# Eleven late node tiles behind the edge pairs of layer 2, expert weights split in place, a new buffer map

## The chip, the cores and the metric

One core of one Trainium2 chip. The metric is the device time of one execution in microseconds (us). Its engines are TensorE (PE, matrix products), VectorE (DVE), ScalarE (ACT), GpSimd (POOL) and SyncE (SP, which only issues transfers here); 16 DMA engines move data between DRAM and SBUF.

## The reference

Two layers of a gated relational graph network over 10000 nodes of 512 features and 5000 edges, then a mixture of experts over the nodes:

```python
for r in range(2):                                  # two relations, w[r] = sum_b att[r, b] * basis[b]
    gate = sigmoid(x_j @ gate_w[r])                 # x_j = x[dst], one row per edge
    msgs.append(gate[:, None] * x_j @ w[r])
msg = where(edge_type == 0, msgs[0], msgs[1])
layer(x) = segment_sum(msg, src) + x @ root + bias
y = relu(layer1(layernorm(x)));  z = layer2(y);  x = x + z
out = x + shared_experts(layernorm(x)) + sum over top 2 of 8 routed experts(layernorm(x))
```

All products are made in about full float32 precision from high and low halves: hi x hi, lo x hi and hi x lo, three matrix instructions per block of 128 of the inner size.

## The kernel before

The nodes are 79 tiles of 128 rows (`NT`; the last is the tail of the 10000 rows and overlaps the one before it). The edges, sorted by relation, are 42 tiles in 21 pairs (`NPAIR`). The five engine programs are written out in order and meet in semaphores. The stages are:

- A: node tiles 0 to 73 of layer 1. Each is normalised, transposed by PE, split (`hi` on ACT, `lo` on DVE), multiplied by the root weights, and `y_out` (DVE) adds the bias into `yout`, which SP stores to the table y1 in DRAM, two tiles in a transfer.
- B: the 21 edge pairs of layer 1. POOL gathers 256 rows (`gather`, L766), ACT and DVE make the gate and the gated halves, PE turns them with a matrix that sums the rows of equal source in the pair (L1119), multiplies by the relation's weights, ACT writes `message`, and POOL scatters it onto y1 with an accumulating indirect transfer (`scatter`, L781). A pair's scatters wait until the pair before it has landed, and a message waits for the scatter two pairs back.
- late A: node tiles 74 to 78 of layer 1 behind the pairs. Their rows of y1 are set to zero at the start; POOL adds the tiles to them with accumulating transfers (L819, L822) once all scatters have landed.
- C: all 79 node tiles of layer 2 (input y1, output stored to the table z), and D: the 21 edge pairs of layer 2, scattered onto z.
- the groups: 20 groups of 512 nodes (the last has 384). SP loads z and x, POOL (`add_x`; for group 0 DVE) adds them, DVE and POOL make the moments, ACT normalises (`q_norm`), PE transposes, ACT and DVE split (`q_hi`, `q_lo`), PE makes router logits, hidden layer and output.

In A and C, one relation weight chunk out of 32 is formed on every second tile from a basis load of 960 KB (`load_basis`, `w_rows`, `w_evac`), goes to DRAM (`store_w`), comes back in two loads into `wrl` and is split at tiles 68 to 71 (`W_SPLIT_AT`, `w_hi`, `w_lo`). In the last steps of A and C (`LEADS`) the first pairs of the next stage are prepared.

Behind D, the kernel loads the two expert weights (1280 KB each) into a staging buffer that takes the place of `xin` and `yout`, ACT and DVE split them in the last five pairs of D and behind it, DVE makes the bias rows (L1541 to L1545) and the router's tables (L1549 to L1558), and every engine waits for all scatters of D (`scattered`). SP issues the loads of x groups 0 and 1 (1024 KB each) right behind the expert weights, at the start of D, and those of z behind the scatters.

Chunks are counted from 0 to 63 over both layers; chunk 34 is the third of layer 2.

Of the kernel before, what the change touches and what calls it, by code (L numbers as in the profile page):

```python
# [20 lines left out]
F32 = mybir.dt.float32  # L21
# [7 lines left out]
P = 128  # L29
# [32 lines left out]
def gnn_moe_kernel(nc, x, src, dst, etype, basis, att, gate_w, root, bias,  # L62
# [3 lines left out]
    KC = H // P  # L66
    NB = basis[0].shape[0]
# [18 lines left out]
    TURN_AT, REPEATS_AT, W_SPLIT_AT = 34, 42, 68  # L86
# [3 lines left out]
    QT = 4  # L90
    QLAST = 3
    LATE = 5
    NA = NT - LATE
    assert NA % 2 == 0 and LATE < 8
    A0, B0, L0, C0, D0 = 0, NA, NA + ET, NT + ET, 2 * NT + ET
    SA, SB, SL, SC, SD = "A", "B", "late A", "C", "D"
    NSTORE = [16 * ((NA // 2 + 1) // 2), 16 * (NA // 4)]

# [8 lines left out]
    with ctx:  # L107
# [75 lines left out]
        w2h, e3 = place("w2h", [P, FC, H], F32R, at=e2)  # L183
        w2l, e4 = place("w2l", [P, FC, H], F32R, at=e3)
# [15 lines left out]
        assert s1 <= top[0]  # L200
        xy_at = top[0]
        xin = sb("xin", [P, 4, 2, H])
        yout = sb("yout", [P, 2, 2, H])
        stage_w1, s3 = place("stage_w1", [P, KC, FH], at=xy_at)
        stage_w2, s4 = place("stage_w2", [P, FC, H], at=s3)
        assert s4 <= top[0]
# [4 lines left out]
        xn_e = sb("xn_e", [P, 4, H])  # L211
        eh, el = sb("eh", [P, 2, H], F32R), sb("el", [P, 2, H], F32R)
        same = sb("same", [P, 2, 2, PW], F32R)
        msg = sb("msg", [P, 4, H])
        stage1, s2 = place("stage1", [P, KC, H], at=xe_at)
        assert s2 <= top[0]
        scratch = sb("scratch", [P, H])
# [3 lines left out]
        top[0] = late  # L221
        xr = sb("xr", [P, 2, QT, H])
        assert top[0] <= root2_end
        zr = sb("zr", [P, 4, QT, H])
        tn = sb("tn", [P, QT, H])
        tth, ttl = sb("tth", [P, 2, KC, QT * P], F32R), sb("ttl", [P, 2, KC, QT * P], F32R)
        gel = sb("gel", [P, 2, QT * P])
        gsc = sb("gsc", [P, 2, QT * P])
        gth, gtl = sb("gth", [P, FC, QT * P], F32R), sb("gtl", [P, FC, QT * P], F32R)
        cwt = sb("cwt", [P, 2, QT * P], F32R)  # L230
        gwp = sb("gwp", [P, KC, P], F32R)
        lgs = sb("lgs", [P, QT, NE])
        lgt = sb("lgt", [P, QT * P])
# [17 lines left out]
        assert top[0] <= nc.sbuf_usable_end, (top[0], nc.sbuf_usable_end)  # L251
# [42 lines left out]
        s_late = sem("late_rows_added")  # L294
# [68 lines left out]
        def phase_of(S):  # L363
            for name, t0, t1 in ((SA, 0, NA), (SL, NA, NT), (SC, 0, NT)):
                if START[name] + t0 <= S < START[name] + t1:
                    return name, S - START[name]
# [1347 lines left out]
```

## Time and profile before

| what | value |
| --- | --- |
| median of 3 runs | 1699.88 us (1698.68 to 1703.02) |
| profiled execution, its time | 1702.22 us |
| profiled execution, its span | 1700.5 us |
| PE busy | 1586.2 us, 93% of the span |
| DVE, ACT, POOL busy | 911.4, 725.0, 510.6 us |
| moved by DMA | 271.47 MB, mean 160 GB/s |

The span is the time between the first and the last instruction of the profile. Busy times of different engines overlap; only what lies on the chain that ends last makes the time. Matrix instructions overlap as well: one of 512 columns is busy for 0.39 us, but one starts every 0.23 us.

### The profile page before, as it was taken

The page shows a single profiled execution, that of the slowest core. Times are in us where ns is not written, and L with a number is a line of the kernel's source. Part 1 is how long each engine was busy: PE and PEld are TensorE (multiplying, and loading weights), DVE is VectorE, ACT ScalarE, POOL GpSimd, SP SyncE. Part 2 cuts the span into 40 slices and gives each one's busy share as a digit, 9 for nine tenths or more (in the row PEclk, how much of TensorE's full clock was granted, in tenths as well). Part 3 has the DMA queues.
Part 4 walks back from the last instruction along what each step waited for, and adds up shares of the span by engine and source line. Part 5 has one row for each costly group of instructions (what it writes and reads, how often), then busy time and mean ns, then how long its engine had stood idle before and what let it go on. Part 6 is the DMA issues. An engine that isn't in the chain of part 4 may idle for free. (4 is left out here: it accounts for less than half of the span.)

```text
span 1700.5 us, 23999 instructions
## 1 busy us (share of the span) xinstructions
PE 1586.2 (93%) x7903; PEld 1253.3 (74%) x7903; DVE 911.4 (54%) x2179; ACT 725.0 (43%) x1168; POOL 510.6 (30%) x562
## 2 busy tenths in 40 slices
PE   3998999998998999999999818999999999999998
PEld 2676766787786777778888616888888888888887
DVE  3554686877732333335665436555556555655543
ACT  2343444666631222223665514444444444443542
POOL 3682232477732000000467433122112211221100
PEclk9999999999999999999999959999999999999999
DMA  8997999576759999994777650231122112211201
GB/s 243 281 284 227 304 299 284 157 134 123 130 68 276 284 280 280 276 283 162 214 128 131 92 173 0 102 121 75 75 105 119 74 74 109 114 74 74 87 26 44
DMA packets 72773, 271.47 MB, mean 160 GB/s; under 512 B 12550, under 2 KB 12564, under 8 KB 57570
## 3 DMA queue, kind: packets, MB, share of 16 engines
q1 hardware_dynamic: 51922, 223.59, 41.6%
q0 software_dynamic: 20752, 46.65, 15.0%
q8 instruction: 50, 0.82, 0.2%
q14 instruction: 49, 0.40, 0.1%
HBM read 179.82 MB, written 90.34 MB: 159 GB/s over the span
## 5 line engine op out<-in xcount | busy, mean ns | idle before, releaser
L848 POOL TENSOR_TENSOR zr<-zr,xr 128x2048 f32<-128x2048 f32 (+1 forms) x19 | 89.2, 4699 | 395.6 <-DMA xr<-in_x 395.1
L879 ACT ACTIVATE th<-bank 128x512 fp32r<-128x512 f32 x158 | 94.4, 597 | 185.8 <-PE bank L1106 185.5
L1086 PE MATMUL bank<-tth,w1h 128*128 128x512 f32 (+1 forms) x400 | 164.0, 410 | 0.1
L1086 PE MATMUL bank<-ttl,w1h 128*128 128x512 f32 (+1 forms) x400 | 156.5, 391 | 0.0
L1086 PE MATMUL bank<-tth,w1l 128*128 128x512 f32 (+1 forms) x400 | 155.4, 388 | 0.0
L1086 PE MATMUL bank<-w2h,gth 128*128 128x512 f32 x395 | 155.2, 393 | 0.0
L1086 PE MATMUL bank<-w2h,gtl 128*128 128x512 f32 x395 | 154.7, 392 | 0.0
L1086 PE MATMUL bank<-w2l,gth 128*128 128x512 f32 x395 | 154.3, 391 | 0.0
L1362 DVE SCALAR_TENSOR_TENSOR tl<-bank,th 128x512 fp32r<-128x512 f32 x79 | 54.7, 692 | 179.2 <-ACT th L879 179.1
L1086 PE MATMUL bank<-root1h,th 128*128 128x512 f32 x316 | 133.4, 422 | 5.9 <-DVE yout L1384 4.2
L766 POOL DMA_INDIRECT gx<-y,dst_slot x42 | 45.5, 1084 | 297.0 <-ACT xn_e L899 274.4
L1086 PE MATMUL bank<-root2h,th 128*128 128x512 f32 x316 | 131.9, 417 | 1.8 <-DVE yout L1384 1.2
L1086 PE MATMUL bank<-root1l,th 128*128 128x512 f32 x316 | 126.4, 400 | 0.0
L1086 PE MATMUL bank<-root1h,tl 128*128 128x512 f32 x316 | 125.4, 397 | 0.0
L1086 PE MATMUL bank<-root2l,th 128*128 128x512 f32 x316 | 125.0, 396 | 0.0
L1086 PE MATMUL bank<-root2h,tl 128*128 128x512 f32 x316 | 123.9, 392 | 0.0
L922 ACT ACTIVATE wevac<-bank 128x512 f32<-128x512 f32 x64 | 38.2, 597 | 183.2 <-PE bank L1157 183.2
L1384 DVE TENSOR_TENSOR yout<-bank,bias_b 128x512 f32<-128x512 f32 x157 | 107.1, 682 | 14.1 <-PE bank L1086 5.8
L1020 ACT ACTIVATE gel<-bank,b 128x512 f32<-128x512 f32 (+1 forms) x100 | 68.3, 683 | 108.3 <-PE bank L1086 108.2
L1365 DVE TENSOR_TENSOR tl<-bank,th 128x512 fp32r<-128x512 f32 x79 | 54.5, 690 | 111.3 <-ACT th L879 110.6
L1119 PE MATMUL bank<-same,eh 128*128 128x256 f32 x336 | 83.6, 287 | 12.3 <-issue 8.5
L1590 DVE TENSOR_TENSOR gtl<-gsc,gth 128x512 fp32r<-128x512 f32 (+1 forms) x80 | 79.3, 992 | 21.7 <-ACT gth L1032 16.3
(204 smaller groups left out, 3790.0 us busy)
## 6 DMA issues: line engine op xcount, KB each, us to landing
basis_t<-in_gnn_basis SPq DMA_DIRECT2D x64, 896.0 KB
xin<-in_x SPq DMA_DIRECT2D x39, 512.0 KB, 8.7
xin<-y SPq DMA_DIRECT2D x39, 512.0 KB, 6.5
z<-yout SPq DMA_DIRECT2D x39, 512.0 KB, 6.9
xr<-in_x SPq DMA_DIRECT2D x19, 1024.0 KB, 6.8
zr<-z SPq DMA_DIRECT2D x19, 1024.0 KB, 4.8
out<-zr SPq DMA_DIRECT2D x19, 1024.0 KB, 3.9
y<-yout SPq DMA_DIRECT2D x37, 512.0 KB, 9.2
```

Of the source, the lines that this page charges most:

```text
L766: pool.indirect_dma_start(out=gx[:, e % 6, :], out_offset=None, in_=x if pr.phase == SB else y1, in_offset=bass.IndirectOffsetOnAxis(ap=ds ...
L848: pool.tensor_tensor(zq, zq, xr[:, q.mod(2), 0:n, :], ALU.add).then_inc(s_zx, 1)
L879: act.activation(th_a[:, s, :], tpb[s][:], f).then_inc(s_hi, 1)
L922: act.activation(wevac[:, u.mod(2), c.mod(2), :], wb[c.mod(2)][:], ACT.Copy).then_inc(s_wv, 1)
L1020: act.activation(gel[:, u % 2, 0:n], outb[u % 2][:, 0:n], ACT.Gelu, bias=b1[:, c:c + 1]).then_inc(s_ge, 1)
L1086: ins = pe.matmul(out_ap, a(k), b(k), start=first, stop=last)
L1119: pe.matmul(o, eh[:, j, k * P:(k + 1) * P], m, start=j == 0, stop=False)
L1362: ins = dve.scalar_tensor_tensor(out=tl_a[:, s, :], in0=tpb[s][:], scalar=0.0, in1=th_a[:, s, :].bitcast(F32), op0=ALU.max, op1=ALU.subtract)
L1365: ins = dve.tensor_tensor(tl_a[:, s, :], tpb[s][:], th_a[:, s, :].bitcast(F32), ALU.subtract)
L1384: dve.tensor_tensor(target, outb[st.T.mod(2)][:], bias_b[st.layer][:], ALU.add).then_inc(s_y, 1)
L1590: dve.tensor_tensor(gtl[:, c, 0:n], source, gth[:, c, 0:n].bitcast(F32), ALU.subtract).then_inc(s_gl, 1)
```

## The change

Layer 2 now treats its last tiles as layer 1 does, but eleven of them (tiles 68 to 78, stage E, `late2_steps`). Stage C ends with tile 67. E's tiles are transposed and multiplied behind the pairs of D, and their results are written to four pair buffers (two of `yout`, `xn_a`, a new `late_out`; the fifth pair takes the first again once its transfer has landed; the tail goes to `scratch`). POOL adds them to z with five accumulating transfers of 512 KB and one of 32 KB. The rows of z from 8704 on, which get only such additions, are zeroed by 13 transfers issued by SP behind stage A and the first basis loads of layer 2. Two of layer 2's weight chunks are formed before C (`FORMED`), the other 30 on its first 60 tiles, and the split moves to tiles 64 to 67. The expert weights are loaded into the places of `w1l` and `w2h` and split there, w1 in D's last five pairs and w2 in E's first five tiles; bias rows, router tables, the addition of x to z for group 0 and its moments stand in DVE's program behind tiles 5, 6, 7 and 8 of E (counted from 0). SP issues x loads 0 and 1 once the last edge rows of D are gated. The group buffers get new places, so that they don't overlap what E still uses.

```diff
-    LATE = 5
-    NA = NT - LATE
+    LATE, LATE2 = 5, 11
+    NA, NC = NT - LATE, NT - LATE2
+    FORMED = [0, 2]
-    TURN_AT, REPEATS_AT, W_SPLIT_AT = 34, 42, 68
+    TURN_AT, REPEATS_AT, W_SPLIT_AT = 34, 42, [68, 64]
-        w2h, e3 = place("w2h", [P, FC, H], F32R, at=e2)
-        w2l, e4 = place("w2l", [P, FC, H], F32R, at=e3)
+        w2l, e3 = place("w2l", [P, FC, H], F32R, at=e2)
+        w2h, e4 = place("w2h", [P, FC, H], F32R, at=e3)
+        stage_w1, _ = place("stage_w1", [P, KC, FH], at=e1)
+        stage_w2, _ = place("stage_w2", [P, FC, H], at=e2)
-        zero_rows = [(y1, r) for r in range(NA * P, N + PW, P)] + [(z, r) for r in range(N, N + PW, P)]
+        zero_rows = [[(y1, r) for r in range(NA * P, N + PW, P)], [(z, r) for r in range(NC * P, N + PW, P)]]
+        late2_steps = [Step(SE, Pos(t)) for t in range(NC, NT)]
+        LATE2_PAIRS = range(NC // 2, NG)
+        def late2_buffer(g):
+            k = (g - NC // 2) % 4
+            return (yout[:, k % 2, :, :], k) if k < 2 else ((xn_a, late_out)[k - 2][:, :, :], k)
+        def late2_added(eng):
+            for k in range(5):
+                eng.wait_ge(s_late2[k], 16 * (len(LATE2_PAIRS[k::4]) if k < 4 else 1))
 # SP
+                    for c in range(FORMED[1]):
+                        sp.wait_ge(s_w, CS + c + 1)
+                        load_basis(1, Pos(c + 2))
+                    store_w(1, Pos(0))
             for c in range(2):
                 load_basis(1, Pos(c))
+            zero_late_rows(1)
             walk(sp, SC, step)
 ...
                 sp.wait_ge(s_mm, D0)
-                for i in range(2):
-                    sp.wait_ge(s_ystore[i], stored(i, 1))
 ...
+            sp.wait_ge(s_xn, 2 * ET)
+            sp.wait_ge(s_el, 2 * ET)
             for q in range(2):
                 load_x(Pos(q))
+            for g in range(NG - 1, NG + 1):
+                sp.wait_ge(s_tp, Step(SE, Pos(2 * (g - 4) + 1)).T.k + 1)
+                load_pair(SE, Pos(g))
             scattered(sp, 1)
             for q in range(2):
                 load_z(Pos(q))
             load_group(Pos(2))
+            late2_added(sp)
 # POOL, behind edges(SD) and scattered(pool, 1)
+            def add_late2(g):
+                rows, k = late2_buffer(g)
+                pool.wait_ge(s_y, NT + 2 * g + 2)
+                pool.dma_start(pair_rows(z, Pos(g), 2), rows, accum_op=ALU.add).then_inc(s_late2[k], 16)
+            for g in LATE2_PAIRS[:4]:
+                add_late2(g)
             group_rstd(Pos(0))
             add_x(Pos(1))
+            for g in LATE2_PAIRS[4:]:
+                add_late2(g)
+            pool.wait_ge(s_y, 2 * NT)
+            pool.dma_start(z[TAIL + again:N, :], scratch[again:P, :], accum_op=ALU.add).then_inc(s_late2[4], 16)
             group_rstd(Pos(1))
 # ACT
+            for c in range(FORMED[1]):
+                w_evac(Pos(CS + c))
             hi(Step(SC, Pos(0)))
 ...
+            hi(late2_steps[0])
             message(Pair(SD, NPAIR - 1), 1)
-            scattered(act, 1)
+            for i in range(LATE2):
+                if i + 1 < LATE2:
+                    hi(late2_steps[i + 1])
+                if i < FC:
+                    expert_hi(FC + i)
             q_norm(Pos(0))
+            late2_added(act)
             for k in range(KC):
                 q_hi(Pos(0), k)
 # PE
+            for c in range(FORMED[1]):
+                w_rows(Pos(CS + c), 1)
             transpose(Step(SC, Pos(0)))
 ...
+            transpose(late2_steps[0])
+            for st in late2_steps:
+                if not is_tail(st):
+                    transpose(Step(SE, st.t + 1))
+                multiply(st)
             scattered(pe, 1)
+            pe.wait_ge(s_y, 2 * NT)
             pe.wait_ge(s_ewl, 2 * FC)
             pe.wait_ge(s_qs, 1)
 # DVE
+                if st.phase == SE and st.g.k - 4 in LATE2_PAIRS and not apart:
+                    dve.wait_ge(s_late2[0], 16)
 ...
-            dve.wait_ge(s_mm, D0 + ET)
-            for n in range(FC, 2 * FC):
-                expert_lo(n)
 ...
+            lo(late2_steps[0])
+            for i, st in enumerate(late2_steps):
+                if not is_tail(st):
+                    lo(Step(SE, st.t + 1))
+                y_out(st)
+                if i < FC:
+                    expert_lo(FC + i)
+                elif i == FC:
+                    bias_rows()
+                elif i == FC + 1:
+                    router_tiles()
+                elif i == FC + 2:
+                    add_first()
+                elif i == FC + 3:
+                    q_stats(Pos(0), range(QT), True)
+            late2_added(dve)
             for k in range(KC):
                 q_lo(Pos(0), k)
```

## Rows read from the trace of the kernel before

**Rows 1.** The page's head: span and instructions.
```profile
span 1700.5 us, 23999 instructions
```

**Rows 2.** Chain that ended last, 930 to 1060 us: start, us, what.
```profile
989.15 5.16 DMA z<-msg,scat_slot
...
994.37 5.67 DMA zr<-z
...
1012.54 0.61 ACT tth L1013
```

**Rows 3.** Waits of PE, 800 to 1060 us: in total, times, longest.
```profile
PE bank L1213 <- ACT tn L1004: 38.4, 2, 36.9
```

**Rows 4.** Windows: length, busy PE, PEld, DVE, ACT, POOL; clock; DMA share; GB/s.
```profile
980.00:990.00 10.00, 0.00 (x0) 0.00 (x0) 1.01 (x2) 0.00 (x0) 4.93 (x4) 0.50 0.52 58
```

**Rows 5.** Timeline of DVE, stage C: start, us, line, operation, [idle before].
```profile
740.36 0.68 DVE L1384 TENSOR_TENSOR yout<-bank,bias_b 128x512 f32<-128x512 f32 x1
...
747.92 0.68 DVE L1384 TENSOR_TENSOR yout<-bank,bias_b 128x512 f32<-128x512 f32 x1
...
783.29 0.68 DVE L1384 TENSOR_TENSOR yout<-bank,bias_b 128x512 f32<-128x512 f32 x1
...
802.51 0.68 DVE L1384 TENSOR_TENSOR yout<-bank,bias_b 128x512 f32<-128x512 f32 x1
```

**Rows 6.** Timeline of POOL: a pair's first scatter, stages B and D.
```profile
335.93 1.68 POOL L781 DMA_INDIRECT y<-msg,scat_slot  x1 [0.31 <-issue]
...
354.35 1.64 POOL L781 DMA_INDIRECT y<-msg,scat_slot  x1 [1.13 <-issue]
...
504.26 1.55 POOL L781 DMA_INDIRECT y<-msg,scat_slot  x1 [4.54 <-issue]
...
819.13 1.64 POOL L781 DMA_INDIRECT z<-msg,scat_slot  x1 [4.73 <-DMA z<-yout]
...
841.83 1.63 POOL L781 DMA_INDIRECT z<-msg,scat_slot  x1 [4.25 <-issue]
...
987.28 1.56 POOL L781 DMA_INDIRECT z<-msg,scat_slot  x1 [4.46 <-issue]
```

**Rows 7.** C's start: a window as in rows 4, and the DMA list's tail add.
```profile
520.00:523.00 3.00, 3.00 (x15) 2.42 (x15) 0.18 (x1) 0.60 (x1) 0.00 (x0) 0.88 1.07 277
...
y<-xn_e POOLq DMA_DIRECT2D x1, 32.0 KB, 13.5
```

**Rows 8.** Timeline of SP's queue, start of D.
```profile
818.40 0.40 SPq L567 DMA_DIRECT2D stage_w<-in_w1T  x1
...
819.40 1.07 SPq L633 DMA_DIRECT2D xr<-in_x  x2
```

**Rows 9.** Timeline of ACT, end of D: the last pair's first message.
```profile
976.03 0.60 ACT L915 ACTIVATE msg<-bank 128x512 f32<-128x512 f32 x1 [4.89 <-DMA z<-msg,scat_slot]
```

**Rows 10.** Timeline of DVE behind D.
```profile
978.39 0.42 DVE L1541 CAST b2r<-b 128x512 fp32r<-128x512 f32 x1
...
980.30 0.75 DVE L1544 SCALAR_TENSOR_TENSOR b2r<-b2lo,lo_row,b2r 128x512 fp32r<-128x512 f32 x1
...
994.47 0.09 DVE L1549 MEMSET topv<- 128x32 f32 x1 [13.42 <-DMA z<-msg,scat_slot]
...
996.26 0.09 DVE L1558 MEMSET cw<- 128x40 f32 x1
...
1000.17 2.50 DVE L1671 TENSOR_TENSOR zr<-zr,xr 128x512 f32<-128x512 f32 x4 [3.82 <-DMA zr<-z]
...
1005.21 0.38 DVE L1571 BATCH_NORM_AGGREGATE qmv<-qbn 128x2 f32<-128x6 f32 x4
```

**Rows 11.** Timeline of POOL: z plus x of group 1.
```profile
1008.19 4.51 POOL L848 TENSOR_TENSOR zr<-zr,xr 128x2048 f32<-128x2048 f32 x1
```

**Rows 12.** Chain that ended last: the same piece of two groups in a row.
```profile
1054.26 3.45 PE bank L1086 x15
...
1088.12 3.45 PE bank L1086 x15
```

More of the change, by code:

```diff
@@ L66, in gnn_moe_kernel @@
     KC = H // P
+    QT = 4
     NB = basis[0].shape[0]
@@ L294, in gnn_moe_kernel @@
         s_late = sem("late_rows_added")
+        s_late2 = [sem(f"late_rows_added{i}") for i in range(5)]
         s_gx = [sem(f"gathered{i}") for i in range(6)]
@@ L367, in phase_of @@
             return None, 0
[L369 to L370 removed]
+        START = {SA: A0, SB: B0, SL: L0 - NA, SC: C0, SD: D0, SE: E0 - NC}
+        NODES_BEFORE = {SA: 0, SL: 0, SC: NT, SE: NT}
         PAIRS_BEFORE = {SB: 0, SD: NPAIR}
[L372 to L373 removed]
+        LAYER = {SA: 0, SB: 0, SL: 0, SC: 1, SD: 1, SE: 1}
+        LAST = {SA: NA - 1, SC: NC - 1}
+        STORES = [[(n // 2 + 1 - i) // 2 for i in range(2)] for n in (NA, NC)]
         def stored(i, layer):
[L377 removed]
+            return 16 * sum(STORES[l][i] for l in range(layer + 1))
         def buffer_free(i, gg):
[L381 removed]
+            return gg.div(2).times(16, 16 * (STORES[0][i] - (NG + 1) // 2) if gg.k > NG else 0)
         class Step:
@@ L551, in store_pair, with zero_late_rows @@
                 wait(sp, s_y, n)
-                if tiles == 1:
-                    before_gg = gg + (-1)
-                    sp.wait_ge(s_ystore[before_gg.mod(2)], buffer_free(before_gg.mod(2), before_gg) + 16)
                 table = y1 if phase == SA else z
+                assert tiles == 2
                 sp.dma_start(pair_rows(table, g, tiles), yout[:, gg.mod(2), 0:tiles, :]).then_inc(s_ystore[gg.mod(2)], 16)
+            def zero_late_rows(layer):
+                for table, r in zero_rows[layer]:
+                    n = min(P, N + PW - r)
+                    sp.dma_start(table[r:r + n, :], zeros[0:n, :]).then_inc(s_zero_rows, 16)
             def flush_stores(phase):
@@ L773, in scatter @@
                         pool.wait_ge(s_sidx, 1)
-                        pool.wait_ge(s_zero_rows, 16 * zero_stores)
+                    pool.wait_ge(s_zero_rows, 16 * sum(len(zero_rows[l]) for l in range(pr.layer + 1)))
                     for i in range(2):
@@ new lines, in router_tiles @@
+            def router_tiles():
+                scattered(dve, 1)
+                dve.memset(topv[:], -1.0)
+                for k in range(KC):
+                    dve.tensor_copy(gwp[:, k, :], zeros[:, 0:P])
+                for i in range(2):
+                    ins = dve.tensor_copy(cwt[:, i, :], zeros[:])
+                link(ins)
+                link(dve.tensor_copy(gwp[:, :, 0:NE], gw[:]))
+                dve.tensor_tensor(gwp[:, :, NE:2 * NE], gw[:], gwp[:, :, 0:NE].bitcast(F32), ALU.subtract)
+                dve.memset(cw3[:, :, 0:2, :], 1.0)
+                dve.memset(cw3[:, :, 2, :], 0.0).then_inc(s_qs, 1)
+                dve.wait_ge(s_qs, 1)
```

159 lines of the change are left out of this document (72 added, 87 removed).

## The prediction, made before the result was known

> **What bounds the kernel now.** I began with the page's span and engine totals [rows 1] and then followed the chain that ended last from its end. The chain is TensorE (PE) work back to 1012.54 us, and before that a row of scatters into z, ending with the one issued at 989.15 that takes 5.16 us; then the first z load, 5.67 us [rows 2]. The waits say what PE did meanwhile: one wait of 36.9 us ahead of the first router transposes [rows 3], and the window inside it shows no PE work and the clock at 0.50, the lower of its two levels [rows 4]. So there are two kinds of stretch. Node tiles (stage C) and expert groups are bound by PE: two C tiles with a weight chunk take 747.92 - 740.36 = 7.56 us, six without one 802.51 - 783.29 = 19.22, or 3.20 each [rows 5]. Edge pairs (stages B, D) are bound by the scatter queue: 18 periods from 354.35 to 504.26 are 8.33 us each, 18 from 841.83 to 987.28 are 8.08 [rows 6], each the landing of the last scatter plus the issue of the next. What PE has to do in the shadow of that queue is free; what disturbs the queue's transfers is paid in full.
>
> All times below are in the profiled execution: span 1700.5, its own time 1702.22, so 1.7 lies around the span. The median of the runs is 1699.88, 2.3 under the profiled time; I carry the difference over.
>
> **Stage C loses eleven tiles.** 11 x 3.20 = 35.2 us come off PE before stage D [rows 5]; everything from D to its last scatter moves forward by that. The places of the lead steps and of the weight split hang on the end of C and move with it; load and split of the last weight rows keep their three tiles of distance. The split now ends on C's last tile, before the first pair, where seven tiles lay between. DVE's two subtractions there come ahead of its work for pair 0, but that waits for PE's turns anyway: nothing, at worst 1.3 us.
>
> **Two chunks formed before C.** Each costs PE 7.56 - 6.40 = 1.16, and they land where PE waits at the layer change, so up to -2.3. But SP also issues their successors' loads (960 KB each, 2.0 MB together) some 12 us earlier, into the stretch in which the y loads and the three accumulating transfers already fill the engines (share 1.07 and 277 GB/s) and in which the last of those adds takes 13.5 us to land [rows 7]. 2.0 MB at 277 GB/s is 7.1 us of queue. Chunk 34's load must be there one tile after C starts, and bias additions of C wait for the adds. Bounds of the stall: 0 (it fits in the time PE spends on tiles 0 and 1) and 7.1; I take 3.0, since only part of the queue stands ahead of what is waited for.
>
> **Thirteen zero stores.** z from row 8704 on is zeroed: 3.2 MB behind stage B's first pairs (before, two transfers of z were zeroed at the kernel's start, where they cost nothing visible). How much bulk traffic slows the scatter queue has two rows. In B, 2.0 MB of basis loads run beside the first two periods, which take 354.35 - 335.93 = 18.4, 1.8 over two normal ones. In D, the expert weights and x groups 0 and 1 (4.7 MB) are issued at 818.4 to 820.5 [rows 8], and the first two periods take 841.83 - 819.13 = 22.7, 6.5 over [rows 6]. That is 0.9 to 1.4 us per MB; 3.2 MB give 2.9 to 4.5. I take +4.2; the bounds are 0 and 11.5 (queue stopped for 3.2 MB at 277 GB/s). No slack gives it back: the next periods are latency.
>
> **x loads moved to the end of D.** SP no longer issues them at the start of D: 2.1 MB x 1.4 = -3.0. It issues them when the last edge rows are gated, about 958.5 in old time, with five scatters to go: +3.0. Net 0, bounds -3 and +3. Dropping SP's wait for the last store ahead of the expert loads moves them by under 2 us. Expert splitting in place halves ScalarE's and VectorE's work per pair in D, which is hidden there.
>
> **Eleven late tiles.** In old time, D's last but one message is at 976.03 [rows 9]; with one expert split, hi and lo behind it PE starts the first late product at 978.5 and ends tile i at 981.4 + 3.2 i. VectorE (DVE) has 1.4 us of its own per tile, plus 0.7 of expert split up to tile 4, bias rows behind tile 5 (978.39 to 981.05: 2.7), router tables behind tile 6 (1.9), z plus x behind tile 7 (2.5) and the moments of group 0 behind tile 8 (2.9) [rows 10]. Played through in order, DVE falls behind PE from tile 7 on: y of tile 8 is written at 1009.5, the moments stand at Q = 1012.4 instead of 1005.6, tile 10's product ends at 1015.9 instead of 1013.4. The waits put in between should be met: the scatters end at 994.3, z's first load lands 5.7 (rows 2) to 13.5 later, 1008.0 at worst against 1005.7 when it is read; the first add, whose buffer tile 8 takes, lands by 1008 if it takes as long as in layer 1.
>
> **What ScalarE and DVE wait for now.** GpSimd (POOL) runs: adds 0 to 3, rstd of group 0, z plus x of group 1, add 4, tail add. rstd ends 2.65 after Q (1005.60 to about 1008.2), at 1015.0; the addition takes 4.5 [rows 11] to 1019.6; two issues bring the last to 1020.9. The first turned group may be written to SBUF only when all adds have landed. PE can do just two transposed banks before. Landing, bounds: 4.8 (a scatter with nothing beside it; 5.16 in rows 2) and 13.5 (layer 1 with its bulk loads, rows 7). Here SP has nothing queued but z and x of group 2, issued 12 us earlier, so I take 5.6: 1026.5. Against 1012.54 [rows 2] that is +14.0, with ends of +13.2 and +21.9.
>
> The Trainium skill ("DMA: Bandwidth & Descriptors", section "Anatomy of one DMA — SWDGE (gpsimd) path") puts a GpSimd transfer at about 2.0 us plus bytes at 436 GB/s, 3.2 us for 512 KB. By that page the wait would end near 1024 and the sum would be some 2.5 us lower. Rows 7's 13.5 us for 32 KB shows it is no bound beside other traffic.
>
> Behind that, router start-up and groups are the same instructions; the clock was low there before and is again after the short gap.
>
> **Sum.** -35.2 (tiles) - 2.3 (chunks) + 3.0 (crowding at C's start) + 4.2 (zeros) - 3.0 + 3.0 (x loads) + 14.0 (start of the router) = -16.3. Profiled time 1702.2 - 16.3 = 1685.9; median 1699.9 - 16.3 = 1683.6, say 1684.
>
> **Rivals.**
> A. The transfers are hidden: zeros and crowding cost 0, x loads gain 3 at D's start and cost nothing at its end: -35.2 - 2.3 - 3.0 + 13.2 = -27.3, median 1673. For it: the C stage has PE busy throughout although DMA is near full. Against: both first-period rows of the scatter queue.
> B. The transfers cost what the crowded rows say: crowding 7.1, last adds 13.5: -35.2 - 2.3 + 7.1 + 4.2 + 21.9 = -4.3, median 1696. For it: rows 7. Against: nothing bulky is queued beside the last adds.
> C. Slower than before: the new buffer map makes the steady expert groups slower, for example through operands of PE, DVE and POOL that now lie elsewhere. A group takes 1088.12 - 1054.26 = 33.86 with PE never idle [rows 12], and there are 20. With -16.3 elsewhere it decides from 0.82 us per group on; at 1.0 it gives +20 - 16.3, median 1704. Against it: PE, the bound, has only its instruction stream to spend there, and that is unchanged.
> D. The change doesn't do what it says: late tiles don't run beside the scatters because a product waits (for y of tile 8 and its buffer, or for the scatter wait in DVE's tables). If the four tiles from tile 7 on waited till behind the adds, 4 x 3.2 = 12.8 would come back: -3.5, median 1696. DVE's order makes a part of this likely (2.5 us is in the sum), not all.
>
> **How the numbers follow.** Forecast 0.58 (its own range 1678 to 1691); A 0.20; B 0.09; D 0.07; C 0.06. A measurement of this kernel tells about 0.3% (5 us) from no change. Slower: C, 0.06. Within 0.3% (over 1694.8): B and D reach their price only when several bounds meet, so half of each, 0.08. Faster 0.86. The range 1670 to 1696 takes in A and B at their own values and leaves out C, the far side of B and D and what lies below A, together under 0.2.
>
> **What would show it.** PE's long wait ahead of the router transposes falls from 36.9 to a few us, followed by a new one of 6 to 9 us before the transposed group's first split, released by the adds. B's first three scatter periods grow by about 4 us in sum; D's first two shrink by 3. C starts with a PE wait for a basis chunk or for y, 3 us. Late tiles run 3.2 us apart up to tile 6. The forecast fails if scatter periods in B stay long after the zeros, if C shows waits for basis throughout, if the last adds take 13 us, or if the group period isn't 33.86.

## The result, and the profile after

| what | before | after |
| --- | --- | --- |
| median of 17 runs each, us | 1701.43 (1695.84 to 1706.84) | 1695.01 (1682.36 to 1701.80) |
| ratio of the times | | 0.9954 (0.9941 to 0.9967) |
| profiled execution: its time, its span | 1702.22, 1700.5 | 1694.41, 1692.7 |

The change is faster, by 0.46% or 7.8 us; 16.3 us had been forecast. The sign was right, the size twice too large. The same kernel against the same kernel before in a second session gave 0.9941 (0.992 to 0.9962), 10.0 us.

The head of the page after, then POOL's timeline with the scatters that answer to [rows 6]: first scatter of the first, third and last pair of B, and the same of D.

```profile
span 1692.7 us, 24017 instructions
```
```profile
335.11 1.68 POOL L814 DMA_INDIRECT y<-msg,scat_slot  x1 [0.20 <-issue]
...
356.88 1.64 POOL L814 DMA_INDIRECT y<-msg,scat_slot  x1 [3.36 <-issue]
...
503.05 1.55 POOL L814 DMA_INDIRECT y<-msg,scat_slot  x1 [4.25 <-issue]
...
791.02 1.63 POOL L814 DMA_INDIRECT z<-msg,scat_slot  x1 [5.50 <-issue]
...
810.03 1.62 POOL L814 DMA_INDIRECT z<-msg,scat_slot  x1 [1.75 <-issue]
...
958.35 1.55 POOL L814 DMA_INDIRECT z<-msg,scat_slot  x1 [4.32 <-issue]
```

These six starts, ACT's first split of the transposed group 0 (the tth of [rows 2]), DVE's subtraction `gtl` that opens the second group, and the span cut every kernel of this study into the same stretches. D0 is the first pair of stage D, "last" the last pair:

| kernel | span | B: first to third | B: third to last | B last to D0 | D0 to D last | D last to split | split to group | groups |
| --- | --- | --- | --- | --- | --- | --- | --- | --- |
| before | 1700.5 | 18.4 | 149.9 | 314.9 | 168.2 | 25.3 | 57.1 | 630.8 |
| before, once more | 1700.0 | 19.4 | 147.8 | 317.0 | 165.2 | 25.1 | 58.6 | 632.0 |
| gate_before | 1698.2 | 18.8 | 149.6 | 315.8 | 166.4 | 25.2 | 57.5 | 630.8 |
| after | 1692.7 | 21.8 | 146.2 | 288.0 | 167.3 | 40.4 | 59.0 | 634.9 |
| after, once more | 1686.2 | 22.3 | 147.2 | 286.0 | 165.7 | 39.1 | 59.0 | 631.9 |
| gate_after | 1690.4 | 22.5 | 148.7 | 285.5 | 166.5 | 39.1 | 57.5 | 630.8 |
| zeros_early | 1697.8 | 18.7 | 150.8 | 287.9 | 166.6 | 37.6 | 61.7 | 632.8 |
| early_chunks | 1691.0 | 23.4 | 155.0 | 280.8 | 166.5 | 38.8 | 58.9 | 632.3 |
| adds_first | 1685.2 | 22.6 | 144.3 | 285.6 | 167.2 | 35.9 | 59.5 | 632.5 |
| seven_tiles | 1688.3 | 19.6 | 146.5 | 295.5 | 169.3 | 29.8 | 59.1 | 631.9 |
| seven_with_chunks | 1689.6 | 19.7 | 147.9 | 298.4 | 167.6 | 27.8 | 59.2 | 631.3 |
| x_behind | 1689.5 | 22.1 | 147.4 | 286.1 | 165.2 | 38.5 | 59.1 | 634.1 |
| adds_first_gate | 1693.6 | 22.9 | 151.0 | 289.7 | 168.3 | 33.7 | 57.3 | 630.8 |
| all_three | 1687.5 | 23.2 | 148.0 | 288.0 | 165.4 | 38.6 | 56.3 | 630.8 |
| wait_back | 1695.3 | 22.7 | 146.5 | 288.6 | 170.5 | 37.0 | 61.7 | 632.9 |
| adds_first_gate_wait | 1686.9 | 23.0 | 149.7 | 287.8 | 168.3 | 34.6 | 56.7 | 630.7 |

What lies ahead of B is not in the table. It was 334.1 to 335.9 us in the three profiles of the program before, 335.0 to 339.9 in twelve of changed programs and 341.7 in zeros_early, the only one that adds transfers there. So a single span says little and the stretches say more; whether the changed programs really lose a little ahead of B, and to what, stays open. In the first pair of profiles: up to B's last pair -1.2, B to D0 -26.9, D -0.8, the tail +15.1, the first group +1.9, the others +4.1; the sum is the 7.8 us.

**The tail.** The chain that ended last, in the stretch of [rows 2]; then PE's waits, 760 to 1060 us, where [rows 3] had 36.9 in one (columns: total, times, longest).

```profile
988.66 4.49 POOL zr L886
993.15 0.60 POOL z L867
993.75 4.82 DMA z<-scratch
...
998.75 0.61 ACT tth L1053
...
1003.61 3.78 PE bank L1296 x8
```
```profile
PE bank L1268 <- DVE ttl L1632: 7.4, 1, 7.4
```

The long wait is gone, and the one forecast in its place stands there: POOL's addition of z and x, the last two adds behind it, and 4.82 us until the last has landed. From D's last pair to the split it is 40.4, 39.1 and 39.1 us in after, again_after and gate_after; before 25.3, 25.1 and 25.2. That is +14.4, forecast +14.0. Three more programs keep this order of adds and x loads: zeros_early has 37.6, early_chunks 38.8, wait_back 37.0, so +12 to +15 is as much as can be said.

**The start of C.** PE's waits from 505 to 560 us, after:

```profile
PE bank L1205 <- DMA basis_t<-in_gnn_basis: 5.3, 1, 5.3
PE bank L1152 <- DMA xin<-y: 2.3, 1, 2.3
```

before, the same stretch:

```profile
PE bank L1106 <- DMA xin<-y: 4.0, 1, 4.0
```

and a window (columns as in [rows 4]), after, then before:

```profile
526.00:532.00 6.00, 3.10 (x13) 1.44 (x14) 0.69 (x1) 0.68 (x2) 4.56 (x5) 0.50 0.96 202
```
```profile
526.00:532.00 6.00, 5.32 (x27) 4.28 (x27) 2.70 (x5) 1.72 (x3) 4.30 (x5) 1.00 0.87 202
```

PE waits for a basis chunk, for which it did not wait before, and in the pause the granted clock falls to 0.50, the lower level (1.2 GHz), where before it was at 1.00. It is a second fall rather than a new kind of one: at 514 to 520 us the clock was 0.50 before and 0.72 after. Behind the pause the chunk's eight matrix instructions take 1.93 us, before 1.07. DVE's timeline has the cost in one number. The eighth tile of C is written at 551.44 before and 556.37 after:

```profile
551.44 0.68 DVE L1384 TENSOR_TENSOR yout<-bank,bias_b 128x512 f32<-128x512 f32 x1
...
815.57 0.68 DVE L1384 TENSOR_TENSOR yout<-bank,bias_b 128x512 f32<-128x512 f32 x1
```
```profile
556.37 0.68 DVE L1446 TENSOR_TENSOR yout<-bank,bias_b 128x512 f32<-128x512 f32 x1
...
786.27 0.68 DVE L1446 TENSOR_TENSOR yout<-bank,bias_b 128x512 f32<-128x512 f32 x1
```

Counted from B's last pair that is 47.2 and 53.3 us. The three profiles of the program before average 48.2 (47.2 to 49.3), the seven with eleven tiles, zeros and chunks as in the change 53.3 (52.8 to 53.8; after, once more, gate_after, adds_first, x_behind, adds_first_gate, all_three). The two programs with the wait put back, the same up to there, have 54.0 and 52.6. The second row of each is C's last tile: the first scatter of D comes 3.56 us after it before (819.13 - 815.57, and 3.56 in all three profiles), 4.75 after.

### The profile page after: what moved, and what is told of

Its sections match the earlier page's. It is cut to its first block and busy times, and to the rows that moved or that the text cites. A ratio compares the mean times of both kernels' runs of the same rounds, so it can differ in the third digit from the quotient of the medians.

```text
span 1692.7 us, 24017 instructions
## 1 busy us (share of the span) xinstructions
PE 1595.1 (94%) x7903; PEld 1258.1 (74%) x7903; DVE 919.8 (54%) x2179; ACT 723.9 (43%) x1168; POOL 513.5 (30%) x568
## 5 line engine op out<-in xcount | busy, mean ns | idle before, releaser
L1446 DVE TENSOR_TENSOR yout<-bank,bias_b 128x512 f32<-128x512 f32 x152 | 103.7, 682 | 31.5 <-PE bank L1132 14.4
L1646 DVE TENSOR_TENSOR gtl<-gsc,gth 128x512 fp32r<-128x512 f32 (+1 forms) x80 | 87.0, 1087 | 21.7 <-ACT gth L1072 16.3
```

Of the source, the lines that this page charges most:

```text
L1446: dve.tensor_tensor(target, outb[st.T.mod(2)][:], bias_b[st.layer][:], ALU.add).then_inc(s_y, 1)
L1646: dve.tensor_tensor(gtl[:, c, 0:n], source, gth[:, c, 0:n].bitcast(F32), ALU.subtract).then_inc(s_gl, 1)
```

## The experiments

There were fourteen more runs. The two called again are the two programs unchanged, measured a second time. Every row of the table is one execution: that of adds_first_gate took 1695.37 us, the longest of its five, 10 us over their median.

**again_after, again_before**: no edit.

> The changed kernel itself, a second time, to see which of the losses in its first profile come back. Theory 1 (port race): the groups lose time where GpSimd's addition of z and x starts just ahead of VectorE's subtraction gtl<-gsc,gth; which of the two comes first changes from run to run, so the number of groups longer than 33.86 us is another one here (0 to 6) and the stage from the first split tth to the end differs from the first profile's 693.95 us by 1 to 5 us. Theory 2 (buffer map): the new places make groups longer; then the same groups are long by the same amounts. For the start of stage C, both expect PE's wait for a basis chunk again, 4 to 6 us. Ratio 0.994 to 0.997.

> The kernel before a second time, for its profile. Theory 1: one or more groups longer than 33.86 us are possible here too, since only the landing of an x load decides. Theory 2: all groups 33.86 us again. Stage C's start without a wait for a basis chunk, the scatter queue of stage B from its first to its last start 170 us within 2.

Measured: 1691.42 us, ratio 0.9941 (0.992 to 0.9962); the program before 1701.78 in its one execution, beside a median of 1701.47 of its runs in that session. The stretches that come again are the stretch to D0 and the tail. The group stretch was 634.9 and is 631.9: a part of the first profile's loss there comes and goes. B of the program before, first to last pair, took 167.2 us, a little less than the 168 to 172 expected.

**gate_after, gate_before**: POOL adds x to the group three ahead only once the router weights of the next group are known, in either program.

```diff
-                if not missing(q + 3):
-                    add_x(q + 3)
                 if not missing(q + 2):
                     group_rstd(q + 2)
+                if not missing(q + 3):
+                    wait(pool, s_cw3, q.times(1, 2))
+                    add_x(q + 3)
```

> Changed kernel, but GpSimd adds x to z of group q+3 only once the router weights of group q+1 are known, where VectorE has no operation with two SBUF inputs of 512 columns. Theory 1 (port race): no group is longer than 33.86 us, gtl takes 0.69 us everywhere in the loop, the time falls 3 to 5 us against the changed kernel in the same job. Theory 2 (buffer map): the groups stay as long as they were, same time. Rival 3: the later addition makes moments or loads late and costs 1 us or more in every group, slower by 20.

> The kernel before with the same gate on GpSimd's addition. Theory 1: gain of 0 to 3 us, since in its profile no group lost more than 0.1 us but other executions may lose some; its spread over rounds shrinks. Theory 2: no change. Rival 3: slower by 20.

Why this place: in the first profile after, two subtractions of DVE that mostly take 0.69 us took 4.17 and 5.15. DVE's timeline:

```profile
1068.55 4.17 DVE L1646 TENSOR_TENSOR gtl<-gsc,gth 128x512 fp32r<-128x512 f32 x1
...
1100.10 5.15 DVE L1646 TENSOR_TENSOR gtl<-gsc,gth 128x512 fp32r<-128x512 f32 x1
...
1107.14 0.69 DVE L1646 TENSOR_TENSOR gtl<-gsc,gth 128x512 fp32r<-128x512 f32 x1
```

and POOL's, the same stretch:

```profile
1067.56 4.62 POOL L886 TENSOR_TENSOR zr<-zr,xr 128x2048 f32<-128x2048 f32 x1 [28.15 <-DMA xr<-in_x]
...
1100.09 4.61 POOL L886 TENSOR_TENSOR zr<-zr,xr 128x2048 f32<-128x2048 f32 x1 [23.56 <-DMA xr<-in_x]
```

Both times POOL's addition had begun just before, 0.99 and 0.01 us, and DVE's subtraction ended when POOL's was over (1067.56 + 4.62 = 1072.18 against 1068.55 + 4.17 = 1072.72; 1104.70 against 1105.25). The Trainium skill says so ("SBUF — State Buffer", section "SBUF: two separate sides"): a DVE operation with two inputs in SBUF and a GpSimd operation that reads SBUF exclude each other for a whole instruction; the rows agree. Gated, POOL's timeline in gate_after is

```profile
1082.78 4.61 POOL L887 TENSOR_TENSOR zr<-zr,xr 128x2048 f32<-128x2048 f32 x1 [7.70 <-DVEq L1696]
...
1116.64 4.62 POOL L887 TENSOR_TENSOR zr<-zr,xr 128x2048 f32<-128x2048 f32 x1 [7.70 <-DVEq L1696]
```

one group apart (33.86, as in [rows 12]), and the groups take 630.8 us in each gated profile, one of before and four of changed programs (630.7 to 630.8), against 630.8 and 632.0 ungated before and 631.3 to 634.9 in nine ungated profiles of changed programs. So the buffer map costs the groups nothing: what is left is where POOL's addition happens to fall, which hangs on when x lands (its releaser in the row). Ratios: gate_after 0.993 (0.9904 to 0.9955), gate_before 0.9985 (0.9968 to 1.0002). In its session gate_after has 1689.36 us and the changed program 1691.42; 3 to 5 us had been expected, and the two intervals overlap. So the gate's effect is shown in the group stretch, not in the time.

**zeros_early**: the thirteen zero stores are issued at the kernel's start with the others.

```diff
             zero_late_rows(0)
+            zero_late_rows(1)
 ...
-            zero_late_rows(1)
```

> Changed kernel, with the 13 zero transfers to z issued at the kernel's start. Theory 1 (they disturb B's first scatters, but B catches up later): the first two periods of B's scatter queue fall from 22 to 19 us, the following 18 grow from 147 to 149, and B's end moves by 1.5 us or less. Rival (my prediction): B gets 3 to 4 us shorter.

POOL's timeline, first pair, third and last of B:

```profile
341.67 1.67 POOL L814 DMA_INDIRECT y<-msg,scat_slot  x1 [0.20 <-issue]
...
360.37 1.64 POOL L814 DMA_INDIRECT y<-msg,scat_slot  x1 [1.29 <-issue]
...
511.14 1.55 POOL L814 DMA_INDIRECT y<-msg,scat_slot  x1 [4.49 <-issue]
```

The first two periods are back at 18.70 us (before 18.4 to 19.4, with the thirteen stores 21.8 to 23.4 in ten profiles), so the stores cost about 3.6 there. The price does not go by the byte: the programs with seven late tiles issue nine such stores at the same place and have 19.6 and 19.7. And first to last pair takes 169.5 here, 168.0 on average before and 170.0 (166.8 to 173.9) with the stores: over the whole stage at most 2 us are theirs, no more than its own spread. The run is a single execution, 1699.55 us, with 341.67 us gone ahead of B: its time as a whole tells nothing.

**early_chunks**: the two chunks are formed behind the first transposes of late A, and SP loads their successors there.

```diff
 # SP, first step of C: ahead of scattered(sp, 0) and the four load_pair
+                    for c in range(FORMED[1]):
+                        sp.wait_ge(s_w, CS + c + 1)
+                        load_basis(1, Pos(c + 2))
+                    store_w(1, Pos(0))
 # PE (ACT's w_evac likewise)
             transpose(late_steps[0])
+            for c in range(FORMED[1]):
+                w_rows(Pos(CS + c), 1)
```

> Changed kernel, with the two weight chunks formed behind the first transposes of the late tiles of layer 1 instead of right ahead of stage C, so that the loads of the next two chunks (2.0 MB) are issued some 15 us earlier, while only scatters are under way. Theory 1 (crowding at C's start costs about 5 us): no wait of PE for a basis chunk, and the time from the last pair's first scatter of B to the first scatter of D falls from 286 to 288 us to about 281; ratio to before 0.990 or 0.991. Rival: stage C is short of DMA all along (share 0.97), the wait only moves to a later tile, and that time stays at 286. Second rival: the loads slow B's last two scatters, and B gets longer by 2 to 3 us, which takes half the gain.

SP's timeline, then POOL's at the end of B:

```profile
499.92 1.54 SPq L518 DMA_DIRECT2D basis_t<-in_gnn_basis  x4
```
```profile
501.08 1.55 POOL L814 DMA_INDIRECT y<-msg,scat_slot  x1 [4.45 <-issue]
...
513.80 1.55 POOL L814 DMA_INDIRECT y<-msg,scat_slot  x1 [9.31 <-issue]
```

The stretch to D0 falls to 280.8, the shortest of all, -35.1 against before, and C's eighth tile comes 48.0 us after B's last pair, as before the change. But the loads now meet the last scatters of B: one period is 12.72 instead of 8 us, and B from its third pair to its last 155.0 where the other programs with the stores have 144.3 to 151.0. The ratio, 0.9924 (0.9899 to 0.9949), can't be told from again_after's. The 2.0 MB cost some 5 us in either place.

**seven_tiles, seven_with_chunks**: seven late tiles instead of eleven, with all adds ahead of POOL's addition and DVE's work for group 0 behind the tiles; the first forms no chunk ahead of C, the second two.

```diff
-    LATE, LATE2 = 5, 11
-    FORMED = [0, 2]
-    TURN_AT, REPEATS_AT, W_SPLIT_AT = 34, 42, [68, 64]
+    LATE, LATE2 = 5, 7
+    FORMED = [0, 0]                 # seven_with_chunks: [0, 2]
+    TURN_AT, REPEATS_AT, W_SPLIT_AT = 34, 42, [68, 68]      # [68, 64]
 # POOL
+            for g in LATE2_PAIRS:
+                add_late2(g)
 ... (the tail's add)
             group_rstd(Pos(0))
             add_x(Pos(1))
 # DVE, behind the tiles
+            add_first()
+            q_stats(Pos(0), range(QT), True)
+            router_tiles()
```

> Changed kernel, but with seven late tiles of layer 2 instead of eleven, no chunks ahead of C and the split at tiles 68 to 71 as before; all adds are issued ahead of group 0's reciprocal roots, and the router tables behind its moments. Theory 1 (eleven tiles overfill the gap: PE had 36.9 us, they take 35.2 plus a 4 us start, and the last add comes behind them): from B's last pair to D's first scatter 293.5 us (315.9 less 7 x 3.2), from D's last pair to the first split about 27, against 286.5 and 39.5 in the changed kernel: 5 us faster than it, ratio to before 0.990 or 0.991. Rival (each tile moved saves its 3.2 us, so eleven are better): slower than the changed kernel by 12.8 less the 5 of C's start, about 8 us, ratio 0.999.

> The kernel with seven late tiles, now with two weight chunks formed ahead of C (loads of the next two behind the y loads of C's start) and the split at tiles 64 to 67: the chunk part of the change alone, put onto that kernel. Theory 1 (the chunk part loses about 6 us at C's start net of the PE time it saves, whatever the number of tiles): from B's last pair to D's first scatter 300 to 302 us against 295.5, PE waits 4 to 6 us for a basis chunk. Rival (the loss in the changed kernel's stage C comes from the end of C, where 68 tiles leave less room around the loads of the weight rows): 293 to 296.

PE's waits, 930 to 1060 us, in seven_tiles; then 400 to 560 us in seven_with_chunks:

```profile
PE bank L1265 <- ACT tn L1041: 14.3, 2, 12.6
```
```profile
PE bank L1203 <- DMA basis_t<-in_gnn_basis: 4.4, 1, 4.4
```

The last add of 32 KB, from issue to landing, in seven_tiles; then the chain that ended last in seven_with_chunks:

```profile
z<-scratch POOLq DMA_DIRECT2D x1, 32.0 KB, 10.6
```
```profile
986.37 12.50 DMA z<-scratch
...
999.05 0.61 ACT tth L1051
```

seven_tiles has 0.9935 (0.9911 to 0.9958) and ties with the changed program; 0.990 or 0.991 had been expected. From B's last pair to the split, 295.5 + 169.3 + 29.8 = 494.6 us, where the changed program takes 495.7, 490.8 and 491.1. The four tiles (12.8 us of PE) are bought with a tail that is 9.3 to 10.6 us longer and a start and an end of C that are dearer. With seven, PE has the 12.6 us wait again, that is room. The last adds don't come for nothing there either: issued behind the z loads, that of 32 KB took 10.6 us and landed about 1.6 us ahead of the split, and in seven_with_chunks it took 12.50 and the split waited for it. But both programs also have the adds ahead of POOL's addition, which the changed program has not. The nearer partners are the programs with eleven tiles and that order (DVE's order for group 0 still differs): adds_first, adds_first_gate and adds_first_gate_wait take 488.7, 491.7 and 490.6 us over the same stretch, the two with seven 494.6 and 493.9. By the stretches eleven tiles are 2 to 6 us better; the ratios, 0.9912 (0.9887 to 0.9938) and 0.9935, don't tell them apart. The chunks, taken alone, make the stretch to D0 2.9 us longer (298.4 against 295.5): 6.3 up to the eighth tile, of which 3.3 come back later. That 298.4 lies between what the theory (300 to 302) and its rival (293 to 296) had expected. The wait for the basis, 4.4 us, is in seven_with_chunks and not in seven_tiles. Ratio 0.9933 (0.9914 to 0.9953): not to be told from seven_tiles.

**adds_first**: POOL issues the last pair's add and the tail's ahead of its addition for group 1.

```diff
             group_rstd(Pos(0))
-            add_x(Pos(1))
             for g in LATE2_PAIRS[4:]:
                 add_late2(g)
 ... (the tail's add)
+            add_x(Pos(1))
```

> Changed kernel, with GpSimd issuing the last two accumulating transfers ahead of the addition of z and x of group 1 (4.5 us). Theory 1 (the router's start waits for the landing of the last add, which waits behind that addition): the time from D's last pair's first scatter to the first split of group 0 falls from 39 to 40 us to about 36, bounded by tile 10's product; ratio to before 0.992. Rival: the start is bound by the moments and the normalisation of group 0 on VectorE, GpSimd and ScalarE, and nothing changes.

POOL's timeline, then ACT's:

```profile
989.69 0.78 POOL L894 DMA_DIRECT2D z<-scratch  x1 [1.31 <-DVE scratch L1446]
990.25 4.75 POOL L886 TENSOR_TENSOR zr<-zr,xr 128x2048 f32<-128x2048 f32 x1
```
```profile
993.16 1.09 ACT L1053 ACTIVATE tth<-bank 128x512 fp32r<-128x512 f32 x2 [2.65 <-DMA z<-scratch]
```

The tail takes 35.9 instead of 37.0 to 40.4, and ACT goes on 3.5 us after the last add is issued, where it was 5.0. Ratio 0.9912 (0.9887 to 0.9938), the lowest of a single edit, though its interval overlaps with that of again_after.

**x_behind**: the x loads of groups 0 and 1 stand behind the scatters, each after its z.

```diff
-            sp.wait_ge(s_xn, 2 * ET)
-            sp.wait_ge(s_el, 2 * ET)
-            for q in range(2):
-                load_x(Pos(q))
 ...
             for q in range(2):
                 load_z(Pos(q))
+                load_x(Pos(q))
```

> Changed kernel, with the loads of x groups 0 and 1 issued with those of z behind the last scatter. Theory 1 (their 2.1 MB delay one scatter by 3.8 us, from 8.0 to 11.8): D's scatter queue from first to last pair takes 162.5 to 163 us instead of 166.5, and the wait behind it grows by 0 to 2, since x is read 10 us after the scatters: 2 to 4 us faster. Rival: the loads then crowd the adds and z, the first split comes 4 us later, same time.

D takes 165.2 us, where it was 165.7 to 167.3, against the 3.8 us that the loads cost in one period of it. POOL's timeline of the first profile after:

```profile
923.26 1.55 POOL L814 DMA_INDIRECT z<-msg,scat_slot  x1 [3.82 <-issue]
...
935.03 1.55 POOL L814 DMA_INDIRECT z<-msg,scat_slot  x1 [8.37 <-issue]
```

That period is 11.77 us. x_behind has no such period, its others are longer in sum, and D falls by less than the 3.5 to 4 us expected. Ratio 0.9923 (0.9906 to 0.994), no more than again_after's interval allows.

**adds_first_gate, all_three**: the edits of adds_first and the gate together; and x_behind on top.

> Changed kernel with both: last adds ahead of GpSimd's addition for group 1, and the gate on its additions in the loop. Both gains add up: 36 us from D's last pair to the first split, groups of 33.86 us all through (630.8 us from the second group's first subtraction to the end), ratio to before 0.989 to 0.991. Rival: with the shorter start the gate's gain is gone, as adds_first alone (0.991).

> Changed kernel with last adds first, the gate, and the x loads behind the last scatter. Stages: 286.5, 163, 36 to 38, 57.5, 630.8 us; ratio to before 0.987 to 0.989 if theory 1 of x_behind holds, 0.990 if its rival does.

The chain that ended last: the last add in adds_first_gate, in x_behind and in all_three:

```profile
1001.63 3.73 DMA z<-scratch
```
```profile
990.25 5.92 DMA z<-scratch
```
```profile
991.08 9.19 DMA z<-scratch
```

adds_first_gate has 0.989 (0.9872 to 0.9908), 1685.43 us, and all_three 0.9899 (0.9884 to 0.9914), 1685.17 us. Both beat the kernel before and the changed one as it was timed in either session; they tie with each other. In all_three D is 2.9 us shorter and the tail 4.9 longer: the same 32 KB add took 9.19 us instead of 3.73. The windows in which it is under way (columns as in [rows 4]), in all_three:

```profile
994.00:997.00 3.00, 0.00 (x0) 0.00 (x0) 0.00 (x0) 0.00 (x0) 2.40 (x1) 0.50 1.04 320
997.00:1000.00 3.00, 0.00 (x0) 0.00 (x0) 0.00 (x0) 0.00 (x0) 0.00 (x0) 0.50 0.58 117
```

and in adds_first_gate:

```profile
1004.00:1007.00 3.00, 0.00 (x0) 0.00 (x0) 0.73 (x2) 1.09 (x2) 2.95 (x1) 0.73 0.37 59
```

With the x loads behind the scatters the DMA engines are still full (share 1.04, 320 GB/s) while PE and everything else waits for the add; with them in D the queue has run dry. It is rival B's mechanism, set off by another edit.

**wait_back, adds_first_gate_wait**: SP waits for the last z stores of C ahead of the expert loads, as before the change; on the changed program, and on adds_first_gate.

```diff
                 sp.wait_ge(s_mm, D0)
+                for i in range(2):
+                    sp.wait_ge(s_ystore[i], stored(i, 1))
                 sp.dma_start(stage_w1[:], ...
```

> The changed kernel with one line of the old one back: SyncE waits for the last z stores of stage C to land before it loads the two expert weights (2.5 MB). In every changed program the first scatter of stage D starts 4.75 to 5.40 us after the last tile of C is written, before 3.56. Theory 1, the expert loads, issued 0.4 us behind the last store, slow that store, which the first scatter waits for: with the wait it starts about 0.6 us earlier, 4.1 to 4.2 us after the tile; the rest is that the last store is now 512 KB and was 256 KB. Theory 2, only the size of the last store counts: 4.75 stays, and the expert loads come later by 3 us at no gain. Theory 3, DVE's split on C's last tile delays pair 0: 4.75 stays too, and the message itself is late (today it is ready at 788.6, 2.4 us before the scatter starts). The ratio should not differ from the changed kernel's 0.9954 and 0.9941 by more than can be measured.

> The best version so far (last adds ahead of GpSimd's addition, and the additions of x gated by the router weights; ratio 0.989) with the same wait in front of the expert loads. Theory 1: 0.6 us less between the last tile of C and the first scatter, and the first two periods of D as before or up to 1 us longer, since the loads start later: ratio 0.989 within its interval. If the expert loads beside the last store cost more than that, the ratio falls to 0.988; if their later start makes D's first periods longer, it rises to 0.990.

SP's timeline in wait_back, with the last store and the first expert load, then POOL's first scatter of D:

```profile
789.38 0.34 SPq L582 DMA_DIRECT2D z<-yout  x1
792.37 0.40 SPq L597 DMA_DIRECT2D stage_w<-in_w1T  x1
```
```profile
793.18 1.63 POOL L816 DMA_INDIRECT z<-msg,scat_slot  x1 [5.26 <-issue]
```

The scatter comes 4.51 us after C's last tile (788.67) and 4.28 in adds_first_gate_wait. Without the wait it was 4.75 to 4.78 in six profiles with eleven tiles and 5.34 to 5.40 in three. So the expert loads beside the store cost 0.2 to 0.5 at least, the first theory's mechanism and about its size, and some 0.8 stays: the store of 512 KB is seen as landed by SP 3.0 us after its issue. D's first two periods take 19.8 and 20.6 us instead of 18.0 to 19.2, so what the wait gives is given back. Ratios 0.9939 (0.9921 to 0.9958) and 0.9887 (0.987 to 0.9904), 1693.05 and 1684.21 us: no difference to the programs without it. adds_first_gate_wait has the lowest ratio of all, in a tie with adds_first_gate.

## Why the prediction was right in sign and wrong in size

Forecast and measured, step by step. Measured is a mean over profiles of changed programs, less the mean of the three profiles of the program before: for B and C the seven named above, for D five of them (without x_behind and all_three), for the router's start and the groups after, again_after and gate_after, to match the two ungated and one gated of before:

| step | forecast | measured |
| --- | --- | --- |
| B, with the zero stores | +4.2 | +2.0 (170.0 - 168.0) |
| C up to its eighth tile: crowding | +3.0 | +5.1 (53.3 - 48.2) |
| C from there to D0: eleven tiles and two chunks fewer | -37.5 | -34.0 (233.7 - 267.7) |
| D, with the x loads | 0 | +0.4 |
| start of the router | +14.0 | +14.4 |
| first group; the others | 0 | +0.8; +1.3 |
| sum | -16.3 | -10.0 |

The sum agrees with the two ratios (-7.8 and -10.0). It leaves out what lies ahead of B, +2.4 in the seven profiles (337.4 - 335.0). Of the miss of 6.3 us, 5.6 lie in C: 2.1 at its start and 3.5 in the rest. So two terms failed: the crowding at C's start, taken at 3.0 and measured at 5.1, and what happens at C's end, put at nothing, where the saving of 37.5 came out as 34.0. What is left nearly cancels, by luck: B came out 2.2 cheaper than forecast, the groups, put at nothing, 2.1 dearer.

- **Bound by PE in C, by the scatters in B and D: right.** In the first profile after, four late tiles were written by the time the last scatter had landed (966.08) and seven behind it, in what had been PE's wait. The rest of C can be read to the tenth: from the eighth tile to D0 the three profiles before have 267.7 each.
- **Crowding at C's start, "I take 3.0, since only part of the queue stands ahead of what is waited for": the mis-sized term.** It is 5.1, and 6.3 where the chunks are the only difference (eighth tile at 54.3 in seven_with_chunks, at 48.0 in seven_tiles), within the 0 to 7.1 and near the full price of 2.0 MB that I had discounted. The chunks' own products were mostly hidden as forecast: in the first pair of profiles PE's wait for y ahead of C shrank from 4.0 to 2.3 us, 1.7 of the 2.3. But a new wait for the next chunk's basis follows, 5.3 us there and 3.4 to 7.2 in the other programs with chunks loaded at this place, and work at the low clock behind it. In early_chunks the eighth tile stands at 48.0, as before the change, and the 4.7 us are paid in B.
- **"Nothing, at worst 1.3" for the split on C's last tile: right in its bounds; but the end of C lost 1.7 all the same.** Sixth tile from the end to D0: 23.03 us before, 24.7 after (seven profiles, 24.6 to 25.3). seven_with_chunks, where the split ends four tiles ahead of the end of C, has 24.25. So the split costs about 0.4, and 1.2 has another cause: C's last store. Before, the last tile is the tail, alone, a store of 256 KB, which lands in 2.0 us; now it is a full pair of 512 KB with 2.5 MB of expert loads right behind, and D's first scatter waits for it. The forecast let the dropped wait "move them by under 2 us" and did not ask who waits for the store.
- The remaining 1.8 of the 3.5 that this stretch lost (34.0 against 37.5) lie in the main where PE waits for DVE, and DVE for a free `yout`: PE's wait for it from 560 to 800 us is 0.9 to 3.1 us in the seven profiles (mean 1.8), 0.2 to 0.6 before. In the first profile after it is one wait, ended at 760.12. From the eighth tile to D0 seven_with_chunks loses only 1.1 in all (244.1 against 243.0), seven_tiles 2.2 (247.5 against 245.3). DVE's waits, same stretch, in the first profile after (before none, none and 1.4 us):

```profile
DVE yout L1446 <- DMA z<-yout: 7.9, 5, 3.1
```

  Of the 7.9 us, 4.0 stand at 561 to 583 and 3.9 at 749 to 759. The first load of the last weight rows is issued at 739.35; that the stores of the latter are late because of it is argued, not tested.
- **Zeros: price about right, "no slack gives it back" not borne out.** The first two periods grew by 3.6 (4.2 forecast over three), and B's rest got shorter by 1.6 on average, which is within its own spread. In zeros_early, with the stores gone, the rest took 150.8, about as long as the longest with them (151.0). The price per MB was wrong as a rule: nine stores cost 0.7 in the first two periods.
- **x loads: right.** D's first two periods 22.7 -> 19.0 (forecast -3.0), one period at its end 11.77 instead of 8 (forecast +3.0). Neither place was free.
- **Tail: right in its steps, and in its size partly by luck.** DVE's order, POOL's addition in front of the last adds and the wait for them were as forecast. But, counted from D's last pair, the moments of group 0 stood 1.2 to 2.7 us later than played through, and the issue of the last add and its landing (4.82, 5.6 taken) together took 1.5 less. The Trainium skill's figure ("DMA: Bandwidth & Descriptors", section "Anatomy of one DMA — SWDGE (gpsimd) path") gave a tail 2.5 us shorter; the 32 KB add alone took 3.29 to 12.50 us in thirteen profiles, so the measured rows were the better guide.
- **"Behind that, the same instructions": right for the instructions, wrong for the time.** Rival C had the place (the groups) and the wrong mechanism: not the map, but an addition of POOL that meets a subtraction of DVE. Rows 12 showed one undisturbed group; the 5.01 us addition and the 2.28 us subtraction beside it were in the trace of before and I had not asked for them.
- **Rivals.** A (transfers hidden) is refuted by C's start and the tail. B (crowding at its bound) by the tail, but C's start went half of its way, and with seven tiles the last add did take 10.6 and 12.5 us. D did not happen: no tile waited for an add. The median, 1695.0, fell within the range, near its upper end, and outside the 1678 to 1691 of the forecast itself. The second session's 1691.4 lies just beside that.

What stays open: why `yout` comes free late at the end of C with eleven tiles, whether x loads can be placed where neither a scatter nor the last add is under way, and why thirteen zero stores disturb B's start so much more than nine.

## What to carry to other kernels

Work moved into a pause is free only together with the transfers that it sets off: two weight chunks fitted the pause, their successors' 2.0 MB made a new one, and moving both ahead of layer 1's late tiles just charged the scatter queue instead. Place the transfers that something waits for ahead of any computation on the same queue or engine: with that one swap (adds before the addition) the tail took 35.9, 33.7 and 34.6 us in three programs, without it 37.0 to 40.4 (but 38.6 in all_three, where x loads crowd the last add). When a tail is filled with work, count what the last pieces push back: four further tiles, 12.8 us of PE, made the tail 4 to 8 us longer even with the adds first and were worth 2 to 6 us in all. And change one thing when two programs are to be compared: seven_tiles has the swap as well, so its tie with the changed program says nothing about the tiles alone.

## What was new about the chip in these runs

- Bulk traffic slowed GpSimd's scatters wherever it was put: 3.6 us for thirteen zero stores (3.2 MB), but 0.7 for nine, 3.8 us for 2.1 MB of x, 4.7 us (12.72 - 8) for 2.0 MB of basis.
- DVE's 0.69 us subtraction with both inputs in SBUF took 4.17 and 5.15 us behind a GpSimd addition that had begun 0.99 and 0.01 us earlier; a fixed order of the two made the group stretch repeat within 0.1 us between kernels (630.74 to 630.81 us), where they had spread over 4.1.
- The same accumulating transfer of 32 KB landed after 3.29 to 4.93 us in nine profiles, and after 5.92, 9.19, 10.6 and 12.50 in the other four (x_behind, all_three, seven_tiles, seven_with_chunks), in which loads of z or x filled the DMA engines beside it.
